# Second layer's delta attention: the transposed factor of the chunk inverse turned by VectorE in 32 by 32 blocks, and the gate sums of all chunks formed ahead of the loop

## The reference, cut to what matters

```python
beta = jax.nn.sigmoid(bb)
g = -jnp.exp(A_log) * jax.nn.softplus(aa + dt_bias)
alpha = jnp.exp(g)
def step(S, inp):
    q_t, k_t, v_t, beta_t, alpha_t = inp
    S = S * alpha_t[..., None, None]
    kv = jnp.einsum('bhk,bhkv->bhv', k_t, S)
    S = S + jnp.einsum('bhk,bhv->bhkv', k_t, (v_t - kv) * beta_t[..., None])
    o_t = jnp.einsum('bhk,bhkv->bhv', q_t, S)
    return (S, o_t)
```

## Time and profile before

| | |
|---|---|
| median of three runs | 8866.54 us (8864.33 to 8873.16) |
| the profiled execution's own time | 8869.6 us |
| its span | 8867.9 us |
| TensorE, VectorE, ScalarE, GpSimd busy, whole span | 7434.6, 5896.1, 4141.6, 2935.6 us |
| the loop of the second layer's delta attention | about 1040 to 2745 us of the span |

### The profile page before, as it was taken

How to read it: one execution, slowest core, us unless ns; L and a number is a source line. 1 busy time by engine, 2 the same in 40 slices (tenths; PEclk the granted TensorE clock), 3 DMA queues, 4 the chain that set the end, 5 groups by cost and what they waited for, 6 DMA issues and landing times. The chain is left out here.

```text
span 8867.9 us, 296237 instructions
## 1 busy us (share of the span) xinstructions
PE 7434.6 (84%) x129602; PEld 5365.8 (61%) x129602; DVE 5896.1 (66%) x11053; ACT 4141.6 (47%) x6986; POOL 2935.6 (33%) x2152
## 2 busy tenths in 40 slices
PE   7999699999996998988988998998986784756666
PEld 3443588888885665665665665666654453645534
DVE  6664477777776885876876866867865667253266
ACT  3554244444444775765765766756752121111121
POOL 0111022222223773764754755746730000101000
PEclk8998699999998998999999999999998895555556
DMA  0000000000001221221221222212210000000000
GB/s 14 1 1 1 5 5 5 5 5 5 5 3 40 70 73 43 69 72 40 73 65 47 70 59 56 71 50 63 72 30 5 9 0 2 3 2 2 4 0 12
DMA packets 192069, 256.75 MB, mean 29 GB/s; under 512 B 59957, under 2 KB 86452, under 8 KB 189876
## 3 DMA queue, kind: packets, MB, share of 16 engines
q1 hardware_dynamic: 190772, 237.70, 10.1%
HBM read 27.84 MB, written 2.10 MB: 3 GB/s over the span
## 5 line engine op out<-in xcount | busy, mean ns | idle before, releaser
L1764 PE MATMUL wa_front<-w_wqkv,wa_xsT 128*128 128x512 f32 x2000 | 994.8, 621 | 40.1 <-PEq L66 20.3
L1686 POOL TENSOR_TENSOR XNT<-XNT 128x1024 f32<-128x1024 f32 x396 | 937.8, 2368 | 251.2 <-DVE XNT L1870 251.2
L1689 POOL TENSOR_TENSOR XNT<-XNT,wa_rnorm 128x1024 f32<-128x1024 f32 x330 | 627.9, 1903 | 361.9 <-DVE wa_rnorm L1878 361.9
L1867 DVE TENSOR_TENSOR XNT<-wa_front,w_scaled 128x1024 f32<-128x1024 f32 x330 | 393.5, 1192 | 311.1 <-ACT wa_sq L1705 228.8
L1764 PEld LDWEIGHTS wa_front<-w_wqkv,wa_xsT 128*128 128x128 f32 x2000 | 346.3, 193 | 316.9 <-issue 297.4
L446 PE MATMUL a0h_ring<-a0h_QT,a0h_KT 32*128 32x512 f32 (+3 forms) x1536 | 457.5, 567 | 14.2 <-ACT a0h_E L564 10.4
L564 ACT ACTIVATE a0h_E<-a0h_ring 128x512 f32<-128x512 f32 (+1 forms) x640 | 320.6, 555 | 296.7 <-PE a0h_ring L446 295.1
L1705 ACT ACTIVATE wa_sq<-wa_front 128x1024 f32<-128x1024 f32 x335 | 340.1, 1015 | 182.5 <-PE wa_front L1764 182.5
L1870 DVE TENSOR_TENSOR XNT<-wa_front,w_scaled 128x512 f32<-128x512 f32 x660 | 421.0, 679 | 0.0
L1883 DVE TENSOR_REDUCE wa_norm<-wa_sq 128x16 f32<-128x1024 f32 x330 | 398.5, 1207 | 0.0
L1770 PEld LDWEIGHTS wa_front<-consts,XNT 128*128 128x128 f32 x2640 | 299.0, 142 | 124.7 <-issue 62.3
(11 more groups left out here) (659 smaller groups left out, 19547.7 us busy)
## 6 DMA issues: line engine op xcount, KB each, us to landing
wa_v_look<-wa_v_all SPq DMA_DIRECT2D x990, 128.0 KB, 2.4
wa_v_look<-wa_v_all SPq DMA_DIRECT2D x660, 64.0 KB, 2.0
wal_v_look<-wal_v_all SPq DMA_DIRECT2D x198, 128.0 KB, 2.4
wal_v_look<-wal_v_all SPq DMA_DIRECT2D x132, 64.0 KB, 2.0
w_wqkv<-in_L_ffn_Wqkv_dram SPq DMA_DIRECT2D x6, 1024.0 KB, 6.4
w_wo<-in_L_ffn_Wo_dram SPq DMA_DIRECT2D x6, 512.0 KB, 6.9
w_wqkv<-in_L_ffn_Wqkv_dram SPq DMA_DIRECT2D x12, 256.0 KB, 7.9
f2w_raw<-in_L_ffn_w_dram SPq DMA_DIRECT2D x48, 64.0 KB, 1.9
```

Source lines behind the costliest of these rows:

```text
L1686: g.tensor_tensor(rot[:, at], rot[:, at], part[:, at], ALU.add).then_inc(s[summed], 1)
L1689: g.tensor_tensor(rot[:, at], rot[:, at], spread(rnorm[:, at, :], HDW), ALU.mult).then_inc(s[done], 1)
L1764: last = pe.matmul(front[:, first + i, :], xsT[:, slot, :], wqkv[:, (2 * n + i) * 512:(2 * n + i + 1) * 512], start=True, stop=True)
L1867: v.tensor_tensor(rot[:, n], src, cos, ALU.mult)
```

## The change

Both halves of the change are in the second layer's delta attention.

First, T is no longer built by TensorE. grow(n) adds bank 4 to `XTc` for all four small levels and then turns `XTc` into T with one VectorE transpose (32 by 32 blocks, 128 x 4 x 32 elements), which waits for the add. `zt(0)` and the first half of tx(1) to tx(4) are gone. The first T is the transpose of the first `XTc`. The quarter adds into `XT` become one add into `XTc` and, behind its transpose, four quarter copies (`place`); tx(5) waits for these by a semaphore of its own (x4_ready).

Second, the gate sums are formed once in stage `a1z`: three products with all 256 columns of g_all and one exponential over them into `decays` [128, 3, 32, 8], which VectorE and GpSimd read by `of_chunk`. The three products, the exponential and the waits on them leave the loop.

```diff
         with Stage(nc, "a1z") as st:
-            s = st.sems("zeroed")
+            s = st.sems("zeroed sums_ps decays_ready")
+            sums = st.ps("sums", (P, 3, 4 * P))
             with nc.Block(no_gpsimd_drain=True) as block:
+                @block.tensor
+                def _(pe):
+                    for n, m in enumerate((c.upto, c.after, c.ones)):
+                        last = pe.matmul(sums[:, n, 0:TILES * H], m, flat(g_all[:]), start=True, stop=True)
+                    last.then_inc(s["sums_ps"], 1)
+
+                @block.scalar
+                def _(a):
+                    a.wait_ge(s["sums_ps"], 1)
+                    a.activation(decays[:].rearrange("p n t h -> p n (t h)"), sums[:, :, 0:TILES * H],
+                                 ACT.Exp).then_inc(s["decays_ready"], 1)
+                    a.wait_ge(s["decays_ready"], 1)
...
                 def zt(n):
                     if q is None:
                         return
-                    if n == 0:
-                        pe.wait_ge(s["lev0_ready"], q + 1)
-                        if q >= 1:
-                            pe.wait_ge(s["zt_ready"], 6 * q)
-                        blocks_of(bank[1], lev[:, 0], lambda p, b: small[p, SMALL, :], s["zt_ps"])
-                    elif n < SMALL:
+                    if n < SMALL:
                         if n == 1:
                             pe.wait_ge(s["lev_ready"], q + 1)
+                            if q >= 1:
+                                pe.wait_ge(s["zt_ready"], 6 * q)
...
-                        blocks_of(bank[2], XTc, lambda p, b: Zt[p, b, :], s["t_ps"])
                         blocks_of(bank[4], Zt, lambda p, b: XTc[p, b, :], s["x_ps"])
                     elif n == 5:
-                        pe.wait_ge(s["X_ready"], LD * q + 5)
+                        pe.wait_ge(s["x4_ready"], q + 1)
...
-                zt(0)
...
-                if j is not None:
-                    if r is not None:
-                        pe.wait_ge(s["s_used"], r + 1)
-                    if j >= 1:
-                        pe.wait_ge(s["decays_ready"], j)
-                    for n, m in enumerate((c.upto, c.after, c.ones)):
-                        last = pe.matmul(bank[6][:, 0, n * G:(n + 1) * G], m, of_chunk(g_all, j),
-                                         start=True, stop=True)
-                    last.then_inc(s["sums_ps"], 1)
...
-                if j is not None:
-                    a.wait_ge(s["sums_ps"], j + 1)
-                    a.activation(decays[:, j % 3].rearrange("p n b -> p (n b)"), bank[6][:, 0, 0:3 * G],
-                                 ACT.Exp).then_inc(s["decays_ready"], 1)
...
-                    g.wait_ge(s["decays_ready"], r + 1)
-                    g.tensor_tensor(newS[:], S[:], spread(decays[:, r % 3, 2, :], P), ALU.mult).then_inc(s["newS_ready"], 1)
+                    g.tensor_tensor(newS[:], S[:], spread(of_chunk(decays[:, 2], r), P), ALU.mult).then_inc(s["newS_ready"], 1)
...
                 def grow(n):
                     if q is None:
                         return
-                    v.wait_ge(s["T_ready"], LD * q + n)
-                    v.wait_ge(s["t_ps"], LT * q + n)
-                    v.tensor_tensor(T[:], bank[2][:, :, 0:32], T[:], ALU.add).then_inc(s["T_ready"], 1)
                     v.wait_ge(s["X_ready"], LD * q + n)
                     v.wait_ge(s["x_ps"], LX * q + n)
-                    if n < SMALL - 1:
-                        v.tensor_tensor(XTc[:], bank[4][:, :, 0:32], XTc[:], ALU.add).then_inc(s["X_ready"], 1)
-                    else:
-                        for k in range(4):
-                            last = v.tensor_tensor(XT[quarter(k), slot, :, quarter(k)], bank[4][quarter(k), :, 0:32],
-                                                   XTc[quarter(k)], ALU.add)
-                        last.then_inc(s["X_ready"], 1)
+                    v.tensor_tensor(XTc[:], bank[4][:, :, 0:32], XTc[:], ALU.add).then_inc(s["X_ready"], 1)
+                    v.wait_ge(s["X_ready"], LD * q + n + 1)
+                    v.transpose(flat(T[:]), flat(XTc[:])).then_inc(s["T_ready"], 1)
+
+                def place():
+                    for k in range(4):
+                        last = v.tensor_copy(XT[quarter(k), slot, :, quarter(k)], XTc[quarter(k)])
+                    last.then_inc(s["x4_ready"], 1)
...
                 if q is not None:
-                    v.wait_ge(s["zt_ps"], LZ * q + 1)
+                    v.wait_ge(s["lev0_ready"], q + 1)
+                    v.tensor_tensor(XTc[:], lev[:, 0], ident, ALU.add).then_inc(s["X_ready"], 1)
+                    v.wait_ge(s["X_ready"], LD * q + 1)
                     if q >= 1:
                         v.wait_ge(s["T64a_ready"], q)
-                    v.tensor_tensor(T[:], bank[1][:, :, 0:32], ident, ALU.add).then_inc(s["T_ready"], 1)
-                    v.wait_ge(s["lev0_ready"], q + 1)
-                    v.tensor_tensor(XTc[:], lev[:, 0], ident, ALU.add).then_inc(s["X_ready"], 1)
+                        v.wait_ge(s["zt_ps"], LZ * q)
+                    v.transpose(flat(T[:]), flat(XTc[:])).then_inc(s["T_ready"], 1)
...
                 grow(3)
                 convolve(1, 0, 2)
                 grow(4)
+                if q is not None:
+                    place()
                 convolve(1, 2, T0)
```

More of the change, by code:

```diff
@@ L903, in l1_attention_stage @@
         eps = outer.sb("eps", [P, 1])
+        decays = outer.sb("decays", [P, 3, TILES, H])
         with Stage(nc, "a1z") as st:
-            s = st.sems("zeroed")
+            s = st.sems("zeroed sums_ps decays_ready")
+            sums = st.ps("sums", (P, 3, 4 * P))
             with nc.Block(no_gpsimd_drain=True) as block:
+                @block.tensor
[9 more added lines that the diff above has]
+                    a.wait_ge(s["decays_ready"], 1)
                 @block.vector
@@ L918, in l1_attention_stage @@
             delta_chunk_steps(nc, st, X, xnt4, c, d, w, raw_w, taps, half_norm, S, hist, g_all, beta_all, nb_all, XT, T64, xs,
-                              eps, small)
+                              eps, small, decays)
 SMALL = 5
@@ L930, in delta_chunk_steps @@
 def delta_chunk_steps(nc, st, X, xnt4, c, d, w, raw_w, taps, half_norm, S, hist, g_all, beta_all, nb_all, XT, T64, xs, eps,
-                      small):
+                      small, decays):
     four, tiny = [P, G, P], [P, G, 32]
     conv = st.sb("conv", [P, 3, 2, G, P])
-    decays = st.sb("decays", [P, 3, 3, G])
     msq, std, rstd = (st.sb(n, [P, G]) for n in ("msq", "std", "rstd"))
@@ L945, in delta_chunk_steps @@
     bank = [st.ps(f"bank{n}", (P, G, P)) for n in range(8)]
-    s = st.sems("xs_ready raw_ps raw_copied conv_ready hist_kept ga_ready sums_ps decays_ready dt_ps E_ready sb_ready "
+    s = st.sems("xs_ready raw_ps raw_copied conv_ready hist_kept ga_ready dt_ps E_ready sb_ready "
                 "strict_ready incl_ready gram_ps N_ready Nc_ready lev0_ready lev_ready zt_ps zt_ready t_ps T_ready "
-                "T64a_ready T64b_ready x_ps X_ready x5_ready x6_ready ktok_ps ktok_ready vtok_ps vtok_ready z_ps tanh_ready "
+                "T64a_ready T64b_ready x_ps X_ready x4_ready x5_ready x6_ready ktok_ps ktok_ready vtok_ps vtok_ready z_ps tanh_ready "
                 "gatez_ready qk_ps AT_ready kS_ps qS_ps qS_used R_ready u_ps u_ready uend_ready o_ps o_done s_ps "
@@ L952, in delta_chunk_steps @@
     QC = 1
-    LZ, LT, LX, LD = 7, 5, 6, 5
+    LZ, LX, LD = 6, 6, 5
     CHUNKS = HEADS1 * BLOCKS
@@ L957, in of_chunk @@
     def of_chunk(x, t):
-        return x[:].rearrange("p (b t) h -> p b t h", b=G)[:, :, t % BLOCKS, t // BLOCKS]
+        return x.rearrange("p (b t) h -> p b t h", b=G)[:, :, t % BLOCKS, t // BLOCKS]
     def weights(t):
@@ L1120, in _ @@
                 if r is not None:
-                    pe.wait_ge(s["decays_ready"], min(step, CHUNKS))
                     pe.wait_ge(s["conv_ready"], 2 * r + 2)
@@ L1235, in evict_z @@
                         return
-                    a.wait_ge(s["zt_ps"], LZ * q + n + 1)
+                    a.wait_ge(s["zt_ps"], LZ * q + n)
                     if LX * q + n >= 2:
@@ L1297, in _ @@
                 if q is not None:
-                    a.wait_ge(s["t_ps"], LT * q + 5)
+                    a.wait_ge(s["t_ps"], q + 1)
                     a.activation(T64[quarter(1), :, 0:32], bank[2][quarter(1), :, 0:32], ACT.Copy).then_inc(s["T64b_ready"], 1)
@@ L1341, in _ @@
                     g.tensor_tensor(sb[:], c.strict.unsqueeze(1).broadcast_to(four),
-                                    spread(of_chunk(nb_all, j), P), ALU.mult).then_inc(s["sb_ready"], 1)
+                                    spread(of_chunk(nb_all[:], j), P), ALU.mult).then_inc(s["sb_ready"], 1)
                 if j is not None:
@@ L1366, in _ @@
                 if r is not None:
-                    beta = spread(of_chunk(beta_all, r), P)
-                    decay = [spread(decays[:, r % 3, n, :], P) for n in range(2)]
```

(2 more changed lines are left out.)

2 lines of the change are left out of this document (1 added, 1 removed).

## The result

The changed kernel takes 8717.81 us at the median of four runs (8713.77 to 8733.7), the kernel before in the same comparison 8869.85 us (8864.33 to 8878.49): a ratio of 0.9831, 95% interval 0.9814 to 0.9848. It is 152 us faster; forecast were 157 us and 8710 us. The profiled execution took 8718.5 us with a span of 8716.4 us, 151.5 us less than that of before.

A forecast was written before the change was run, and what follows sets the result against it. TensorE's queue, in program order, was taken as the bound. Gains of 64.7 + 24.3 (zt(0)) + 76.8 + 6 = 171.8 us less 15 lost gave 156.8 net, so 8710 us; range 8688 to 8765, 8 in 10.

The forecast's parts named there:

- the pairs: Four groups of tx a step lose their first half on TensorE, each giving back 0.30 us: 76.8 us gained.
- The wait for yT: Output product ahead of zt(1) waits for ScalarE's yT: 0.1 us a step, 6 us lost.
- The first T: Ahead of zt(1): add into XTc (0.59 us) and transpose end in time, at about 1453.10 to 1453.40 against 1453.99.
- T at the levels: Longer path to T inside grow: free where VectorE is idle, some 0.1 us late at level 2, 6 us lost.
- The copies (`place`): Quarter copies ahead of tx(5): nothing lost at 0.287 us each, up to 0.6 us a step at 0.589.
- rival A: VectorE becomes the bound; SBUF operations double beside GpSimd, late T and copies give 74 us back: 8784 us, chance 0.11.
- The gate sums: Sums leave TensorE's queue between zt(6) and tx(6), mostly over a wait: 0.1 us a step, 6 us gained (0 to 12).
- The sums ahead of the loop: Forming the sums and exponential once for all chunks ahead of the loop: 3 us lost, of 0 to 5.
- B: TensorE's wait on the mask levels only moves to zt(1), so 64.7 us don't come: 8774 us, chance 0.05.
- C: Slower because VectorE's transpose is slow, 256 us per further microsecond; at 1.4 us about 8951 us, chance 0.03.
- D: TensorE's granted clock falls to one half for the stage; time could reach 9700 us, chance 0.02.
- three signs that I named for being wrong: Transpose over 0.5 us; zt(1) now waits; VectorE has no idle time left between tx(2) and tx(3).

The follow-up runs named there:

- lev0_dve: Changed kernel with level 0 of the masks multiplied by VectorE and GpSimd's other levels waiting for VectorE's identity add: 8716.99 us, 0.9828 of the kernel before.
- turn_twice: Changed kernel with each of the four transposes of grow done twice: 8785.22 us, 0.9911 of the kernel before.
- newS_gap: Changed kernel with GpSimd's newS, same place in its queue, waiting until VectorE has written y: 8673.7 us, 0.9797 of the kernel before.
- zt0_only: Kernel before with only zt(0) taken out, the first T now a VectorE transpose of the first XTc: 8800.02 us, 0.9929 of the kernel before.

## Why the prediction was right, point by point

The forecast of 8710 us met 8718, for the reason given: TensorE's queue sets the step, and it got rid of 1.94 - 0.44 = 1.50 us at `zt(0)` (forecast 1.47) and 4 x 0.30 us in the pairs (forecast 0.30). That is the mechanism, and it held. That 152 us lie so close to 157 is in part luck: the loop alone gave 146, and the smaller terms were off in both directions and in part cancelled:

- **The wait for yT**, put at 6 us, cost nothing. The profile shows 31.0 us of it, but the projection of K to u is 1.75 us in all four columns: in the kernel before, the same weight loads stood 29.9 us in "issue".
- **The first T** was said to be in time. I priced the add at the 0.589 us of the earlier trace rows, a mean that was the rest of GpSimd's operation seen from one start time. It started earlier, took 1.345, and `zt(1)` was late by 0.07 us and its own pitch grew by 0.03 (0.38 to 0.41): some 6 us. lev0_dve shows that cause; in it both pitches are back at 1.09 and 0.38.
- **T at the levels**: forecast 6 us at level 2 alone. It is 0.04 at level 1 and 0.08 at level 2, 0.12 x 64 = 8 us. At levels 3 and 4, where VectorE is free, T is there 1.24 and 1.27 us after the start of `tx`, as against the 1.30 of the sum. At level 1, where the prediction had nothing in the way, `o` (L1429) stands ahead of the add, and T comes after 1.46. turn_twice shows the path to be real.
- **The copies (`place`)** were put at 4 x 0.287 us and hidden; that is the term that was mis-sized most. One of the four stands behind `Estrict`, the four take 1.95 us, and `tx(5)` waits: 1.20 to 1.41, 0.21 x 64 = 14 us. The same block was named in rival A with 0.5 us a step as its upper end.
- **The gate sums**, put at 6 us, gave 2.3. `tx(6)` does come 0.21 us earlier (1.37 to 1.16), and `kS` to yT takes it back whole (1.14 to 1.35). I had `y` gain half of it, on the picture of shared bandwidth. `y` ends 0.54 behind newS, before (1475.52 and 1476.06, for `y`) as after, and newS comes in GpSimd's queue behind the operation that waits for AT, which the sums don't move. newS_gap, which takes newS out of the way, bears it out.
- **The sums ahead of the loop**, put at 3 us of 0 to 5: from the first clearing of stage `a1z` to the first operation of the loop's stage are 4.8 us after and 3.3 before, so 1.5 us.

In all: 1.50 + 1.20 - 0.10 - 0.12 - 0.21 = 2.27 us a step, and 26.18 - 23.91 = 2.27 were measured. Of the rivals, B didn't happen (zt0_only). A is there in part, 89% busy and three kinds of blocked operation: the copies stand and the transposes don't, as it had by the rule that it cites. But the late T and copies together cost (0.10 + 0.12 + 0.21) x 64 = 28 us and not 74. C had the right slope: 256 us for each microsecond of transpose was said, 68 / 0.34 = 200 were measured, slack at two levels included. D did not: the clock is 1.00.

What I said would show it held, with two exceptions: the copies lie above 0.35 on the mean, and the waits for T are 26.5 us and not under 10, at levels 1 and 2. Of the three signs that I named for being wrong, two came, though small: `zt(1)` waits, 0.19 us in the step shown and 0.07 more than before by the pitch, and between `tx(2)` and `tx(3)` VectorE is idle for 0.07 us of 3.0 at the median (0.15 before). The first says rightly that the first T is late; the second was so nearly true before the change that it tells little.

## What to carry to other kernels

Cost a removed group by its pitch in the queue that sets the end, and put no value on it where another engine's result stands behind it anyway: 0.76 us of gate sums a step were worth 0.04. A duration read beside a busy neighbour is not a price: if an operation ends at a fixed distance behind the neighbour's end, moving it earlier makes it longer and nothing else. Look then for a gap in which the neighbour blocks nobody; one added wait on GpSimd was worth 33 us here, beside the 146 us of the whole change.

## What the runs showed of the hardware that was not expected

A VectorE operation with two inputs in SBUF that runs into a GpSimd operation on SBUF ends 0.15 us (128 columns) or 0.55 us (512 columns) behind GpSimd's, whatever its start: 1.345 us for 0.29 us of work, 1.54 in most steps for 0.69. The copy from SBUF to SBUF of 32 x 128, with one input, stands as well, but only the one of the four that runs into it: 1.29 us, 0.08 behind, where the others take 0.17 to 0.24. A GpSimd operation that starts behind a VectorE one with two inputs in SBUF stands in the same way: level 0 of `lev` takes 0.86 us for 0.45 and ends 0.31 behind `ga`; levels 1 to 4, in newS_gap, 1.71 for 1.27 and 1.13 behind. In all five cases the distance behind the neighbour's end is 0.14 us less than what the operation takes alone (0.29 - 0.15, 0.69 - 0.55, 0.22 - 0.08, 0.45 - 0.31, 1.27 - 1.13): by an estimate from these, about 0.14 us of it go by before it has to stand.

The 32 by 32 transpose of 128 x 128 fp32 took 0.31 us in all 320 cases, also where GpSimd was at work: `L1416` at 1471.53 ran beside GpSimd's `sb` (L1335, from 1471.30 for 1.10 us), and 65 of the 320 lie wholly inside a GpSimd operation.
